# Third scores ahead of the out projection in an adaLN block with attention and experts

## The reference, cut to what matters

```python
for l in range(4):
    res = x
    h = rms(x, ln1[l])
    q, k, v = rope(h @ wq[l]), rope(h @ wk[l]), h @ wv[l]      # 16 heads, 4 kv heads, 64 wide
    attn = softmax(q @ k.T / 8 + causal)
    x = clip(res + (attn @ v) @ wo[l], -100, 100)
    res = x
    h = rms(x, ln2[l])
    comb = top-2 of 8 experts, from softmax(h @ wr[l])
    x = clip(res + sum_e comb[e] * ((silu(h @ wg[l, e]) * (h @ wu[l, e])) @ wd[l, e]), -100, 100)
```

## Time and profile before

| | |
|---|---|
| median of 3 runs | 3354.49 us |
| lowest, highest | 3334.46, 3355.78 us |
| the profiled execution | 3336.53 us |
| its span, first to last instruction | 3334.7 us |
| mean granted TensorE clock in the span | 0.91 |

### The profile page before, as it was taken

The page is one execution under the profiler, slowest core; times in us unless marked ns, Lnnn a source line. Parts: engine busy times, 40 slices in busy tenths (PEclk is TensorE's granted clock), DMA queues, the critical chain, the costliest instruction groups (busy, mean ns, idle before and its releaser), DMA issues.

```text
span 3334.7 us, 66162 instructions
## 1 busy us (share of the span) xinstructions
PE 2653.1 (80%) x20406; PEld 2128.6 (64%) x20406; DVE 2285.3 (69%) x8164; ACT 2001.3 (60%) x7080; POOL 1860.3 (56%) x1662
## 2 busy tenths in 40 slices
PE   5317888999789977988789977988789977989572
PEld 2216666777577765777677766776677766777462
DVE  6786766677776777766776677767776677766343
ACT  3017776776666766666666666666666665666320
POOL 0026776555766576556665575555765575555403
PEclk9659999999999999999899998999999998999665
DMA  9211222664266624553275524553266524552574
GB/s 367 117 46 64 79 89 89 209 212 137 74 207 213 203 79 152 186 179 117 80 234 199 181 83 155 188 174 111 93 217 202 183 74 141 177 183 93 173 249 127
DMA packets 287021, 511.54 MB, mean 153 GB/s; under 512 B 39968, under 2 KB 159296, under 8 KB 286144
## 3 DMA queue, kind: packets, MB, share of 16 engines
q1 hardware_dynamic: 270288, 473.72, 41.8%
q0 software_dynamic: 16384, 33.59, 3.2%
HBM read 316.58 MB, written 106.69 MB: 127 GB/s over the span
## 4 chain that ended last, share of the span: by engine, by line
PE 35%; DVE 29%; ACT 14%; POOL 13%; issue 5%; DMA 2%; SPq 2%; DVEq 0%; POOLq 0%
ACT arena L1055 6%; PE psum L784 6%; PE psum L759 5%; POOL arena L1308 4%; PE psum L802 4%; DVE arena L1572 4%; DVE arena L1593 4%; POOL arena L1275 3%; DVE arena L1563 3%; ACT arena L1063 2%; POOL rows_in L1299 2%; DVE arena L1591 2%; PE psum L804 2%; PE psum L902 2%; PE psum L832 2%
## 5 line engine op out<-in xcount | busy, mean ns | idle before, releaser
L1055 ACT ACTIVATE arena<-arena 128x128 f32<-128x128 f32 (+1 forms) x2048 | 902.3, 445 | 58.1 <-DVE arena L1597 58.1
L1308 POOL TENSOR_TENSOR arena<-arena 128x512 f32<-128x512 f32 (+1 forms) x512 | 745.3, 1475 | 238.3 <-DVE arena L1602 238.3
L1323 POOL TENSOR_TENSOR arena<-arena 128x512 f32<-128x512 f32 x320 | 401.5, 1281 | 478.1 <-DMA arena<-arena 477.9
L1063 ACT COPY arena<-psum 128x384 f32<-128x384 f32 x1024 | 446.9, 482 | 302.7 <-PE psum L784 299.7
L784 PE MATMUL psum<-arena 128*128 128x128 f32 x3072 | 479.4, 295 | 162.7 <-ACT arena L1063 108.8
L784 PEld LDWEIGHTS psum<-arena 128*128 128x128 f32 x3072 | 349.6, 147 | 286.5 <-ACT arena L1063 174.9
L759 PE MATMUL psum<-arena 64*128 64x128 f32 (+1 forms) x4096 | 451.5, 361 | 12.7 <-DVE arena L1593 6.2
L1593 DVE CUSTOM_DVE_ANT_0 arena<-psum,arena 128x256 f32<-128x256 f32 x1024 | 429.8, 420 | 0.0
L1572 DVE TENSOR_TENSOR arena<-psum,arena 128x512 f32<-128x512 f32 x640 | 392.6, 677 | 9.7 <-PE psum L834 9.7
L1055 ACT ACTIVATION_READ_ACCUMULATOR arena<-arena 128x1 f32 x2048 | 389.1, 190 | 0.0
L802 PE MATMUL psum<-arena 128*64 128x256 f32 x2048 | 339.0, 411 | 31.3 <-DVE xT_lo L1683 31.3
(11 more groups left out here) (199 smaller groups left out, 5585.2 us busy)
## 6 DMA issues: line engine op xcount, KB each, us to landing
gu<-gu_kept SPq DMA_DIRECT2D x320, 512.0 KB, 4.4
wd<-wd_kept SPq DMA_DIRECT2D x320, 256.0 KB, 4.0
arena<-arena SPq DMA_DIRECT2D x128, 384.0 KB, 3.0
arena<-arena SPq DMA_DIRECT2D x128, 256.0 KB
arena<-rows_in SPq DMA_DIRECT2D x320, 64.0 KB
rows_out<-arena SPq DMA_DIRECT2D x320, 64.0 KB, 2.5
rows_in<-arena SPq DMA_DIRECT2D x34, 512.0 KB, 8.4
rows_out<-arena SPq DMA_DIRECT2D x34, 512.0 KB, 8.2
```

The source lines that it names most:

```text
L1055: ins = A.activation(a, a, ACT.Exp, bias=negmax[:, q, k:k + 1], accum_out=rowsum[:, q, k:k + 1])
L1063: A.copy(probsT[:, 4 * (q % 2) + i, :], psum[:, t_bank(key), 0:3 * P]).then_inc(sem("t_free"), 1)
L1308: ins = G.tensor_tensor(a, a, r[:, :, t:t + 1].broadcast_to([P, 4, P * (t + 1)]), ALU.mult)
L1323: G.tensor_tensor(keys_and_queries(it, u), keys_and_queries(it, u), turned_part[:, u, :], ALU.add) \
```

## The change

On PE and in the numbering of the banks `scores(it, 2)` moves ahead of `project_out(it - 1)` and `turn_h(it + 1)`, directly behind place 2. On DVE `mask_and_max(it, 2)` moves ahead of place 2, and `invert(it, 1)` ahead of `update_x(it - 1)` and `low_h(it + 1)`; before, both stood behind `low_h(it + 1)`. The lists of ACT, POOL and SP stay. The S ring is used in the order scores, out, q/k instead of out, scores, q/k.

```diff
--- before.py
+++ after.py
@@ -177,12 +177,12 @@
         if now:
             t["v", it] = len(t)
         place(it, 2)
+        if now:
+            scores(it, 2)
         if old:
             s["out", it - 1] = len(s)
         if coming:
             t["h", it + 1] = len(t)
-        if now:
-            scores(it, 2)
         place(it, 3)
         if coming:
             qk(it + 1, range(2))
@@ -1728,14 +1728,15 @@
                     invert(it, 0)
                 if old:
                     copy_o(it - 1, 3)
+                if now:
+                    mask_and_max(it, 2)
                 place(it, 2)
+                if now:
+                    invert(it, 1)
                 if old:
                     update_x(it - 1)
                 if coming:
                     low_h(it + 1)
-                if now:
-                    mask_and_max(it, 2)
-                    invert(it, 1)
                 place(it, 3)
                 if coming:
                     rope(it + 1, range(N_QK1))
```

## The result

The changed kernel took 3402.01 us (median of 4 runs, 3381.69 to 3412.30) against 3355.14 for the kernel before in the same set: a ratio of 1.0147 [1.0083, 1.0211], slower where 3331 was forecast, and outside the range. The change makes this kernel slower by about half a per cent.

A forecast was written before the change was run, and what follows sets the result against it. The prediction took a relay between engines, none alone, as the bound. Terms -26.6 - 5.1 + 6.8 + 1.5 = -23.4 us, off the median of 3354.49, gave 3331 us; range 3300 to 3364.

The forecast's parts named there:

- the term for the first nine plain steps: Plain steps without a gather: q/k waits 0.75 us longer for `low_h`, +6.8 us in all.
- `rope` ... starts at 366.6 either way: Plain steps without a gather: `rope`, formerly behind the masks, keeps its start although q/k starts 0.75 us later.
- the clock as a rival: TensorE's clock: a shifted timeline could shorten the slow stretch in most steps, 21 us more gain, 3310 us; chance 0.14.
- The port rival: DVE beside POOL: the second normalising holds `low_h`, making q/k and `rope` late, +34 us, 3389 us; chance 0.08.
- The expert term: 28 full expert steps: earlier gate and `rope` shrink PE's wait at L802, 0.95 us a step, 26.6 us in all.
- taken back later: Expert steps: the gain becomes a wait on POOL or DMA, only losses stay, about +3 us, 3357 us; chance 0.18.
- the steps with it mod 8 = 6: The chain from `rope` to the fourth normalising gains 0.85 us in each of 6 steps, 5.1 us in all.
- q/k in expert steps waiting for `low_h`: Sign against the forecast: in expert steps the q/k projection on PE would be held by `low_h`; no size given.
- DVE's idle before the masks: Sign in full expert steps: the idle before `low_rows` falls from 3.87 to some 1.9 us, placed before the third masks.
- the total at L802: Sign on PE: the total wait of weight loads for the low expert rows falls from 44.5 us to below 15.
- Plain steps with a gather: 18 steps: the later `update_x` is hidden behind the gather's chain, so zero change, bounds 0 and +0.2 us each.

The follow-up runs named there:

- e4: New order only in the 29 steps without expert work at spot 2, old order in the others: 3396.17 us, 1.0159 of the kernel before.
- e1: The changed kernel as it is, run a second time: 3355.95 us, 1.0047 of the kernel before.
- e13: The changed kernel as it is, run once more in a later set: 3355.25 us, 1.0064 of the kernel before.
- e7: e4 plus 20 unused transposes on PE before q/k and POOL waiting for `choose` before `rope_adds`, in plain steps: 3314.00 us, 0.9935 of the kernel before.
- e15: The changed kernel plus unused transposes on PE and POOL's wait for `choose`, both in plain steps, as e12, in another set: 3287.05 us, 0.9837.
- e5: e4 plus 20 transposes on PE in plain steps, results unused, in the gap before q/k: 3331.52 us, 0.9980 of the kernel before.
- e6: e4 plus POOL waiting for the end of `choose` before `rope_adds` in plain steps: 3332.46 us, 0.9985 of the kernel before.
- e2: The kernel before, unchanged, profiled a second time: 3353.93 us in one run.
- e3: New order only in the 35 steps with expert work at spot 2, old order in the others: 3320.02 us, 0.9937 of the kernel before.
- e14: The same kernel as e3, run again in a later set: 3314.46 us, 0.9935 of the kernel before.
- e12: The changed kernel plus unused transposes on PE and POOL's wait for `choose`, both in plain steps: 3336.58 us, 0.9956 of the kernel before.
- set 3: Four kernels run together on one chip: old order with both additions, two variants taking h early with POOL's wait, and e12: 0.9991, 1.0002, 0.9973, 0.9956.

## Why the prediction was wrong

**The step that failed** is the term for the first nine plain steps: "the logits, choosing and fourth masks behind PE slide. +0.75 x 9 = +6.8 us (bounds 0 and 1.0)". It measured 22 to 35 us against the mean of the old order's profiles (38 in e4 against the first one). The two profiles of the changed kernel without late signals lie on either side of its median (3356 and 3355): that of e1 is of an execution of 3371 us and holds 35 us, that of e13 is of one of 3337 and holds 22. Four things went into it:

- The slide itself is 1.1 us, not 0.75 (q/k at 9.37 instead of 8.25). 0.17 of it is a bank. The prediction looked at the banks of the third scores only. The four heads fill all four S banks, and the out projection, next in the ring, must wait for the first third mask: that is the new L852 <- L1593, 0.17 us in most steps and 1.18 in the one shown above from the profile with late signals. With both cures (e7, e15) the first eight steps are 0.7 to 1.3 us longer than in the old order (35.7 to 36.1 in four profiles). That is near the slide of 1.1, and it would be the price of the order alone if the additions themselves cost nothing there, which no run shows.
- "`rope` ... starts at 366.6 either way" was wrong: it hangs on q/k, and started 11.1 us into the step instead of 10.0 (10.45 where q/k ran at full clock, as in e5).
- The idle before q/k went from 1.80 to 2.53 us, and behind it the granted clock was at its lower level. Profiles with late signals left out, in the new order without the busy work (e1, e4, e6, e13) the first twelve q/k matmuls ran slow, wholly or in part, in 30 of 36 such steps; in the old order (before, e2, e3, e14) in 2 of 36, and with the busy work (e5, e7, e15) in none of 27. The prediction had the clock as a rival that could only make it faster: "it can as well cost that" stood there without a price or a chance.
- `choose` slid by 2.5 us (1.1 with the clock full, as in e5), from 2.6 ahead of `rope_adds` into them. The prediction moved the chain and did not ask what each of its operations now stands beside.

**The port rival** had the mechanism right and the victim wrong. It priced `low_h`. In e1 `low_h` kept 0.42 to 0.43 us in 62 of 64 steps; the others are one of 0.90, in step 0, and one of 0.46, together 0.5 us. The other profiles hold at most six longer ones, none over 0.52 apart from that in step 0, and the two of the kernel before none. It was close: in step 28 of e1 `low_h` starts at 1487.78 and the second normalising, which would have held it, at 1488.13. The rival left `choose` out, though the row for it stood in the prediction: the earlier trace rows shows a routing operation held to 1.26 us by `rope_adds`. Its 3389 us at a chance of 0.08 came nearer to the first result than the forecast, for a wrong reason; to the 3356 and 3355 us of the later sets the forecast is the nearer. These two lie inside the prediction's range, but it had the sign wrong: each is slower than the kernel before beside it (3345 and 3336).

**The expert term** was right in mechanism and almost half too large. In step 28 of e1, set beside the earlier trace rows from the start of `project_v` in each (1478.17 and 1434.15): `update_x` 7.31 us in (6.95 foretold, 5.76 before), `low_h` 9.61 (9.2, 7.98), the gate 10.10 (9.8, 10.86), `rope` 11.49 (11.15, 12.20), L802 15.61 (15.4, 16.32). `update_x` comes 0.36 later than foretold (the bank wait of 0.17 and an out projection of 3.81 instead of 3.74 us are 0.24 of it), and the gain at L802 is 0.71 us a step and not 0.95. 28 x 0.71 + 6 x 0.7 = 24 us against 31.7 foretold for both kinds; e3 and e14 measured 0.63 and 0.65%, 21 and 22 us. Nothing of it was taken back later, so that rival falls (its "only the losses stay: about +3 us" also kept the 5.1 us of gain in the steps with it mod 8 = 6; the losses alone are 8.3), and "q/k in expert steps waiting for `low_h`", named as a sign against, is just on the edge: q/k starts at 1488.30 and `low_h` ends at 1488.21. DVE's idle before the masks (1.86 us) and the gate right behind `low_h` came as foretold; the total at L802 fell to 17.8 us and not below 15.

**Plain steps with a gather** were put at zero. In e1 they were +0.7, -0.4 and +1.1 us (mod 8 = 7, 0, 1), together 8 us. Against the mean of the old order's four profiles, which differ by up to 9 us there, the new order is 6 (e1), 12 (e4) and 1 us (e13) longer: too little to tell from none.

**The sum** by what was measured: +22 to +35 in the first nine, +1 to +12 with a gather, -21 in the expert steps, so +2 to +26 us; measured 0.47 and 0.64%, 16 and 21 us. The first result's further 0.8% lies with the late signals, by the comparison of e12 (0.9956, with them) and e15 (0.9837, without), the same kernel. That they caused it is argued from this, not shown by a run that sets them.

## What to carry to other kernels

When an edit shifts a chain, list for each operation in it what it stood beside and what it will stand beside, above all short two-input VectorE operations against GpSimd's long ones: a shift of 2.5 us, of which the edit itself made 1.1, turned 1.4 us of routing into 3.5. A PE gap that an edit lengthened had a second price here in the clock behind it; cheap work in it, or an explicit wait that keeps two engines apart, was worth more than the edit itself. Split an edit, and a cure too, by kind of step before judging it: here a 0.65% gain and a 1.6% loss hid in one number, and more than half of what the cures won lay in steps that the edit had hardly touched.

## What the runs showed of the hardware that was not expected

- Twenty useless transposes (2.35 us of PE) in a gap of 2.53 us took the plain half from 1.0159 to 0.9980, each against the kernel before in its own set, although q/k starts no earlier. 24 us of it lie in the first nine steps, where q/k then ran at full clock in all.
- Small DVE operations in a chain waited out one GpSimd operation after another: the two of L1631 took 1.36 us together instead of 0.26, and L1633 1.19 instead of 0.17, beside `rope_adds` of 1.24 us each; a wait on POOL's side for the end of `choose` was worth 1.7 points on e4, over half of it in steps that had the meeting before the change.
- The signals of PE arrived up to some 2 us late against the matmul records in the first profile of the changed kernel and in all profiles of set 3, whatever the order, and in none of the others. Those profiles, and only those, name a "remote" releaser. With them the changed kernel measured 1.0147, without 1.0047 and 1.0064; the kernel before, timed beside them, had medians of 3355 and 3349 us, against 3336 to 3345 in the other sets. Since one set shared one chip, chip and moment can't be told apart. These traces also lack about a sixth of the semaphore records, so whether the profiler sees the cause or makes part of it stays open too.
